# A graph kernel's edge loop: zero products at its start, attention columns and left-half turns inside it

## The reference

```
h = x @ W + b
adj[row, col] = 1; adj[col, row] = 1; adj += eye; adj /= max(row_sum, 1)
out = dw[0] * h; cur = h
for i in range(3):
    cur = adj @ cur
    out += dw[i + 1] * cur
x = layernorm(x + relu(out))
```

## Time and profile before

| | us |
|---|---|
| median of three runs | 394.62 |
| the profiled execution | 393.99 |
| its span, first to last instruction | 392.1 |
| PE busy | 366.8 (94%) |
| DVE busy | 281.6 (72%) |
| ACT busy | 239.0 (61%) |
| mean granted PE clock | 0.991 |

### The profile page before, as it was taken

One profiled execution on the slowest core, in us unless ns is written; L12 is line 12 of the kernel. 1 busy time (PEld: TensorE's weight loads), 2 busy tenths in 40 slices (PEclk: granted clock), 3 DMA queues, 4 the chain that ended last, 5 costly groups with the idle time before them and its releaser, 6 DMA issues.

```text
span 392.1 us, 7757 instructions
## 1 busy us (share of the span) xinstructions
PE 366.8 (94%) x2704; PEld 215.5 (55%) x2704; DVE 281.6 (72%) x595; ACT 239.0 (61%) x419; POOL 104.1 (27%) x97
## 2 busy tenths in 40 slices
PE   1799998999999999999999999999899999999990
PEld 0344456544444444444444444444358889999990
DVE  7999989729994775206755555564695978999984
ACT  9789998495722255202661011367866999999444
POOL 5611000059910167300792000277200000112110
PEclk9999999999999999999999999999999999999996
DMA  5960006006000000000243000034203111310005
GB/s 179 390 196 3 0 3 214 3 1 216 0 0 2 0 0 3 3 0 2 54 98 63 0 2 2 10 72 80 55 1 112 47 61 59 107 55 3 4 3 217
DMA packets 27446, 22.70 MB, mean 58 GB/s; under 512 B 19536, under 2 KB 19728, under 8 KB 27408
## 3 DMA queue, kind: packets, MB, share of 16 engines
q1 hardware_dynamic: 26544, 19.06, 16.2%
q10 hardware_dynamic: 864, 3.15, 2.4%
HBM read 15.87 MB, written 2.13 MB: 46 GB/s over the span
## 4 chain that ended last, share of the span: by engine, by line
PE 83%; ACT 6%; DVE 6%; issue 2%; DMA 1%; DVEq 0%; POOL 0%; ACTq 0%
PE ps L755 20%; PE ps L1114 14%; PE ps L1055 8%; PE ps L964 7%; PE ps L1005 7%; PE ps L927 7%; PE ps L918 7%; PE ps L788 4%; PE ps L908 4%; PE ps L897 3%; ACT cts L499 2%; PE ps L809 2%; ACT cts L507 1%; DVE adj L1357 1%; PE ps L824 1%
## 5 line engine op out<-in xcount | busy, mean ns | idle before, releaser
L755 PE MATMUL ps<-big,xTs 128*128 128x512 f16 x384 | 84.3, 379 | 0.3 <-DMA xTs<-big 0.3
L755 PEld LDWEIGHTS ps<-big,xTs 128*128 (+1 forms) x384 | 37.0, 98 | 43.9 <-issue 0.4
L664 ACT ACTIVATE big<-big,uvt 128x1024 bf16<-128x1024 f32 x55 | 58.7, 1143 | 0.0
L568 ACT ACTIVATE big<-xcur,nmr,rstd (+1 forms) x24 | 19.5, 813 | 34.0 <-DVE nmr L1383 34.0
L440 POOL TENSOR_TENSOR big<-xcur,big x16 | 18.5, 1156 | 61.3 <-ACT xcur L569 60.3
L788 PE MATMUL ps<-big,xTs 128*128 128x512 f32 x64 | 33.8, 628 | 0.0
L474 ACT ACTIVATE big<-ps 128x512 f16<-128x512 f32 (+2 forms) x17 | 9.7, 568 | 35.3 <-PE ps L755 30.9
L457 POOL TENSOR_TENSOR xcur<-xcur,c 128x512 f32<-128x512 f32 x6 | 7.1, 1183 | 89.4 <-DVE c L1586 89.4
L410 POOL TENSOR_TENSOR big<-xTs,big 128x2048 f16<-128x2048 f32 x4 | 16.2, 4084 | 52.8 <-ACT big L474 52.8
L1055 PE MATMUL ps<-big,cst 128*128 128x260 f16 x256 | 29.8, 275 | 0.0
L964 PE MATMUL ps<-cst,big 128*128 128x512 f16 x128 | 27.8, 379 | 0.1
(11 more groups left out here) (212 smaller groups left out, 689.0 us busy)
## 6 DMA issues: line engine op xcount, KB each, us to landing
big<-u_rows ACTq DMA_DIRECT2D x6, 512.0 KB, 3.7
xTs<-in_xT SPq DMA_DIRECT2D x2, 1024.0 KB, 9.3
xcur<-in_x SPq DMA_DIRECT2D x1, 2048.0 KB, 17.8
out<-xcur SPq DMA_DIRECT2D x8, 256.0 KB, 2.5
big<-in_W SPq DMA_DIRECT2D x1, 1024.0 KB, 6.0
cts<-in_W3T SPq DMA_DIRECT2D x1, 1024.0 KB, 13.3
xTs<-in_W1T SPq DMA_DIRECT2D x1, 1024.0 KB, 5.4
xTs<-in_wc SPq DMA_DIRECT2D x1, 1024.0 KB, 8.2
```

What stands on the lines that cost most here:

```text
L664: act.activation(above[:, a % AHEAD, :], uf[:, h % 2], ACT.Relu, scale=BIG, bias=vb[:, j, h:h + 1]).then_inc(S["above_in"], 1)
L755: return mm(bank, lhs(k)[a], rhs(k)[b], start=start and k == 0 and n == 0, stop=stop and k == KT - 1 and n == 2)
```

## The change

Seven things, in the order of the program:

1. `blank`, a zeroed piece of the W1 slot, feeds 19 matmuls of 128x512 on PE that nobody reads (`warm`): eight first, two and five around the key transposes, two behind each of quads 0 and 1.
2. The products are spread evenly over quads 2 to 26. xT comes in three transfers (the first 128 nodes apart), and the banks of the product tiles are a list.
3. Four column blocks of the attention columns stand behind the products of quads 14 to 17; ACT copies the result (`columns_in`) behind its relu of quad 19. w3t moves from cts to the wn slot.
4. Edge groups from 48 on have window bases of at least 512 (`low`, `first_i[:, 3]`), so columns below 512 are final when window 47 is added.
5. ACT casts the left half of c32 in four pieces behind its last relu, before the loop's end on DVE; PE turns blocks 0 to 3 from it behind quad 31. The right half is cast behind the last add: tiles 0 to 3 by DVE in two pieces, tiles 4 to 7 by ACT.
6. From quad 14 on, DVE makes the lo-hots of quads 16, 21, 26, 31 (before: 15, 21, 27).
7. ACT's squares of w3t come behind the last eviction.

```diff
-H_FROM = 4
-H_TO = 31
-H_LATE = 32
+H_FROM = 2
+H_TO = 27
 LO_TURN = 14
+WARM = (8, 2, 5, 2)
+COLUMNS_FROM = 14
+H_BANKS = (2, 3, 4, 5, 3, 4, 5, 3)
+XT_NODES = ((0, P), (P, HALF), (HALF, N))
...
-CAST_COLS = ((0, 256), (256, 512), (512, 1024))
-CT_BANKS = (0, 1, 5)
+LEFT_GROUP = 48
+CT_BANKS = (2, 5, 2, 5, 0, 1, 2, 5)
...
-            return q > 1 and (q % 2 == 0 if q < LO_TURN else q % 6 != 3)
+            return q > 1 and (q % 2 == 0 if q < LO_TURN else q % 5 != 1)
...
-                return NT * KT * (i - H_FROM) * (i + H_LATE) // ((H_TO - H_FROM) * (H_TO + H_LATE))
+                return NT * KT * (i - H_FROM) // (H_TO - H_FROM)
...
+                if mine[i - 1] < COLUMNS_FROM + KT + 1 <= q:
+                    act.wait_ge(S["wa_done"], 1)
+                    act.wait_ge(S["wba_in"], 1)
+                    copy(abT[:], ps[:, 2, 0:256].rearrange("p (k c) -> p k c", c=64)[:, :, 0:VCOL + H], WSCALE).then_inc(S["columns_in"], 1)
...
+            act.wait_ge(S["win_free"], LEFT_GROUP)
+            for j in range(0, NT, 2):
+                copy(cst[:, j:j + 2, 0:HALF], c32[:, j:j + 2, 0:HALF]).then_inc(S["cst_left"], 1)
...
+            evict_turned(0)
+            evict_turned(1)
+            act.wait_ge(S["win_free"], NG)
+            for j in (4, 6):
+                copy(cst[:, j:j + 2, HALF:N], c32[:, j:j + 2, HALF:N]).then_inc(S["cst_act"], 1)
+            for t in range(2, NT):
+                evict_turned(t)
...
+            def warm(n):
+
+                for _ in range(n):
+                    mm(ps[:, 4, :], blank[:, 0:P], blank, start=True, stop=True)
...
-                    pe.wait_ge(S["acc0"], t - 3)
-                    pe.wait_ge(S["h_lo"], t - 3)
+                    pe.wait_ge(S["acc0"], t - 2)
+                    pe.wait_ge(S["h_lo"], t - 2)
...
+                if q < H_FROM:
+                    warm(WARM[3])
...
-            pe.wait_ge(S["w_in5"], 16)
-            pe.wait_ge(S["small_in"], SMALL)
-            pe.wait_ge(S["h_lo"], 5)
-            pe.wait_ge(S["acc0"], 5)
-            attention_columns(range(KT)).then_inc(S["wa_done"], 1)
+                if q == COLUMNS_FROM:
+                    pe.wait_ge(S["w_in5"], 16)
+                    pe.wait_ge(S["small_in"], SMALL)
+                    pe.wait_ge(S["h_lo"], 1)
+                    pe.wait_ge(S["acc0"], 1)
+                if 0 <= q - COLUMNS_FROM < KT:
+                    attention_columns(q - COLUMNS_FROM)
...
+            pe.wait_ge(S["cst_left"], NT // 2)
+            pe.wait_ge(S["columns_in"], 1)
+            ct_block(0).then_inc(S["ct_done"], 1)
+            pe.wait_ge(S["acc0"], NT - 1)
+            pe.wait_ge(S["h_lo"], NT - 1)
+            ct_block(1).then_inc(S["ct_done"], 1)
+            for t in range(2, 4):
+                pe.wait_ge(S["cts_ready"], t - 1)
+                ct_block(t).then_inc(S["ct_done"], 1)
...
-                if 0 < j < NT - 3:
-                    ct_block(j + 3)
+                if j < 4:
+                    pe.wait_ge(S["cst_act"], 2)
+                    pe.wait_ge(S["cst_dve"], 2)
+                    if j >= 2:
+                        pe.wait_ge(S["cts_ready"], j + 1)
+                    ct_block(j + 4).then_inc(S["ct_done"], 1)
...
+            def cast_right(j):
+                dve.tensor_copy(cst[:, j:j + 2, HALF:N], c32[:, j:j + 2, HALF:N]).then_inc(S["cst_dve"], 1)
+
             dve.wait_ge(S["win_free"], NG)
-            for c0, c1 in CAST_COLS[0:2]:
-                dve.tensor_copy(cst[:, CA:NT, c0:c1], c32[:, CA:NT, c0:c1]).then_inc(S["cst_dve"], 1)
-            for t in range(tiles_low, NT):
-                h_lower(t)
+            cast_right(0)
...
-                if t == 1:
-                    dve.tensor_copy(cst[:, 2:5, c0:c1], c32[:, 2:5, c0:c1]).then_inc(S["cst_dve"], 1)
+                if t == 0:
+                    cast_right(2)
+                    for n in range(tiles_low, NT):
+                        h_lower(n)
```

More of the change, by code:

```diff
@@ L68 @@
 LN16 = 2.772588722239781
-CA = 3
 HT = NT // 2 - 1
@@ L183, in build @@
         base = sb("base", [NG, 1], F32)
-        first_i = sb("first_i", [1, 3, NG], I32)
+        low = sb("low", [NG, 1], F32)
+        first_i = sb("first_i", [1, 4, NG], I32)
         packed = sb("packed", [1, NG // 3 + 1], I32)
@@ L316, in _ @@
             sp.dma_start(w0raw, W0.rearrange("(k p) n -> p k n", p=P)).then_inc(S["w_in0"], 16)
-            for half in range(2):
-                nodes = slice(half * HALF, (half + 1) * HALF)
-                sp.dma_start(xT32[:, :, nodes], xT.rearrange("(k p) n -> p k n", p=P)[:, :, nodes]).then_inc(S[f"xT_in{half}"], 16)
+            for i, (n0, n1) in enumerate(XT_NODES):
+                sp.dma_start(xT32[:, :, n0:n1], xT.rearrange("(k p) n -> p k n", p=P)[:, :, n0:n1]).then_inc(S[f"xT_in{i}"], 16)
             sp.dma_start(w3t, W3T.rearrange("(k p) n -> p k n", p=P)).then_inc(S["w_in5"], 16)
@@ L776, in _ @@
             ins.then_inc(S["tr"], 1)
+            warm(WARM[2])
             def h_part(t, k):
+                if k == 0 and t == 1:
+                    pe.wait_ge(S["xT_in1"], 16)
                 if k == 0 and t == 2:
@@ L818, in far_columns, with attention_columns @@
                 pe.transpose(ps[0:1, 4, 0:NG], far_at[0:NG, 0:1], id32[0:NG, 0:NG]).then_inc(S["tr"], 1)
-            def attention_columns(ks):
-                for k in ks:
-                    for j in range(KT):
-                        ins = mm(ps[:, 2, k * 64:k * 64 + VCOL + H], w3t[:, j, k * P:(k + 1) * P], abT[:, j, :],
-                                 start=j == 0, stop=j == KT - 1)
-                return ins
+            def attention_columns(k):
+                for j in range(KT):
+                    ins = mm(ps[:, 2, k * 64:k * 64 + VCOL + H], w3t[:, j, k * P:(k + 1) * P], abT[:, j, :],
+                             start=j == 0, stop=j == KT - 1)
+                if k == KT - 1:
+                    ins.then_inc(S["wa_done"], 1)
             def attention_bias():
@@ L1204, in link @@
                 dve.wait_ge(S["link"], links[0])
+            dve.memset(blank, 0.0).then_inc(S["blank_in"], 1)
             dve.wait_ge(S["cols"], 2)
@@ L1343, in _ @@
                 dve.wait_ge(S["far_cast"], NT)
+                for t in range(4):
+                    dve.wait_ge(S["far_turn"], t + 1)
+                    dve.tensor_copy(cts[:, t, :], bank16(LEFT_AGAIN[t])).then_inc(S["far_turned"], 1)
+                dve.wait_ge(S["far_turned"], 4)
             dve.wait_ge(S["const_ready"], 12)
-            c0, c1 = CAST_COLS[2]
-            dve.tensor_copy(cst[:, 0:2, c0:c1], c32[:, 0:2, c0:c1]).then_inc(S["cst_dve"], 1)
             for t in range(NT):
```

97 lines of the change are left out of this document (45 added, 52 removed).

## The result

| | before | changed |
|---|---|---|
| median | 394.48 us (394.15 to 397.08, 4 runs) | 398.48 us (396.45, 396.58, 400.38, 400.38) |
| ratio of medians, interval | 1 | 1.0101 [1.0067, 1.0134] |
| profiled execution | 393.99, span 392.1 | 396.58, span 394.7 |
| mean granted clock of it | 0.991 | 0.985 |

The change costs about 1%. The forecast was 395.2 within 391.9 to 398.0; the median lies 0.5 outside. The times lie in steps of about 1.7 us (396.5, 398.3, 400.0 to 400.4); half of the experiments ask what those steps are.

What follows compares the result with a forecast made beforehand. PE was taken to bind the loop up to quad 18, then ACT's chain to step 1. Work removed behind the loop against a loop ending 2.8 later nets +0.6 on the median 394.62: 395.2, range 391.9 to 398.0.

Steps and rivals of the forecast that it cites:

- The sum up to quad 6: Edge loop's start on PE: five products, windows, far columns and one wait after quad 2; quad 6 starts at about 18.0.
- Quad 17's columns: Middle of the edge loop: PE's products, windows and four column blocks from quad 6 sum to 20.8, ending at 38.8.
- ACT's wait: Edge loop, behind quad 19's relu: ACT waits for the columns it copies, 34.85 to 38.85, 4.0 us.
- The last add: End of the edge loop on DVE: 23.6 us of work from 39.05, ending at 62.65.
- First product of step 1: Behind the loop: first product with the adjacency at 66.5, against 65.50 before, with ACT ending the chain.
- The net of +0.6: Up to step 1's second half: it starts at 82.15 instead of 81.51, and all behind shifts alike.
- comparison of tile 0: Behind the loop on DVE: starts at 64.95 after ACT's casts, turns and first eviction; 1.55 before the first product.
- Rival one: Middle of the loop: PE does not bind, ACT's wait vanishes, DVE decides, comparison 3.8 earlier: 391.4; chance 0.24.
- Rival three: Edge loop: DVE's busy time is partly waits, so the loop ends some 2 us before rival one's: 389.4; chance 0.05.
- a new gap behind 82: After step 1's second half starts: nothing new expected; a gap there would be wrong in kind. No size given.
- Rival 2b: Loop's thin end, from about 53.7: clock falls, step 1 starts at 1.2 GHz, 2.2 plus 0.3: 397.7; chance 0.23 with 2a.
- Rival 2a: Loop's start: zeros leave the clock low, five first products cost 0.85 more each, up to 4 us; chance 0.23 with 2b.

Runs made afterwards that it cites:

- e10: The changed kernel timed and traced once more, nothing altered: 400.0 us, ratio 1.0133.
- e6: e2 with H_TO = 29 instead of 27, spreading the 32 products over quads 2 to 28: 395.56 us, ratio 1.0008.
- e1: The kernel before with 51 transposes put into the far branch's body, which is never entered: 397.08 us, ratio 1.0057.
- e2: The changed kernel with 16 more matmuls in the far branch's body, never entered: 396.37 us, ratio 1.0026.
- e4: e2 with ACT's four left casts waiting for the last window instead of window 48: 401.17 us, ratio 1.0157.
- e7: The changed kernel without its 19 products of zeros, 35 unexecuted ones in the far branch keeping the later program's place as in e2: 398.16 us, ratio 1.0086.
- e13: The changed kernel with 5 further products meant for PE's wait near 280, which stood at 300 instead: 400.63 us, ratio 1.0149.
- e16: The changed kernel with the attention loop's first pass written out and 6 products in PE's wait of 1.6 us: 398.2 us, ratio 1.01.
- e14: The kernel before with 5 further products meant for PE's wait near 280, which stood at 300 instead: 395.67 us, ratio 1.0032.
- e17: The kernel before with the attention loop's first pass written out and 5 products in PE's wait of 1.23 us: 394.06 us, ratio 0.998.
- e3: The changed kernel with 16 more executed products of zeros, two behind each of quads 27 to 31 and six ahead of the first turn: 394.62 us, ratio 1.0001.

## Why the prediction was wrong, and where it was right

**Loop and opening: right.** First real product forecast at 11.65 with 0.90; it came at 11.77 with 1.10 (later ones 0.92). The sum up to quad 6 gives 17.75 where the text says about 18.0; it started at 18.14. Quad 17's columns end at 38.59 (38.8). ACT's wait, the row of waits from 8 to 70 us that answers to the earlier trace rows:

```profile
ACT abT L475 <- PE ps L843: 3.1, 1, 3.1
```

3.1 us against 4.0 forecast. The last add, with its row answering to the earlier trace rows:

```profile
62.00 0.50 DVE L1296 TENSOR_TENSOR c<-c,ps 128x328 f32 x1 [0.20 <-DVE c L1296]
```

ends at 62.50 (62.65). First product of step 1 at 66.18 (66.5), L941 at 81.94 (82.15). The net of +0.6 up to here was +0.43.

The order of limits was right, but the closeness at 66.2 is in part luck. ACT began its left casts at 57.63 where the sum had 59.2, and the comparison of tile 0, forecast at 64.95, came 1.2 us sooner:

```profile
63.77 1.23 DVE L1398 SCALAR_TENSOR_TENSOR adj<-cst,cts 128x1024 f16<-128x1024 f16 x1 [0.55 <-ACT cts L475]
```

From there to the first product it took 2.41 us where 1.55 was put (2.18 in e10), and the two misses nearly cancel. DVE had 0.55 us to spare ahead of this comparison, not over 1.

Rival one, PE not binding the middle, fell: PE was busy without a gap from 13.40 to 38.59. Rival three fell with it. The run nearest to it is e6, with ACT's wait down to 0.3: its step 1 started 0.92 earlier (65.26), so the 3.8 us put on this rival look too high.

**The gap: the step that failed.** The sum ended at L908 with +0.6 and took all behind it as a shift. The prediction's last line called a new gap behind 82 "wrong in kind", and this is what came: 2.02 us, shown by e1 and e2 to need only the 51 matmuls that the change adds to PE's program (19 zeros and 32 turns in the unentered body). The prediction priced the order of instructions, and put what their number does to the code behind at nothing. No rival had it. A smaller term was put at nothing as well: PE's wait near 280 is 0.36 longer, 1.58 or 1.59 for ACT in every trace of the changed kernel without a filler there, 1.23 in the kernel before; why is not known.

**The clock: priced, but rated too low and placed once.** Rival 2b said thin work at the loop's end lets the clock fall, 2.5 us, chance 0.23. The fall came in every trace of the changed kernel's loop without extra zeros (the changed kernel, e2, e4 to e7, e10, e13, e16). Where it reached the first products of step 1 (3.57 against 1.89 us, L941 at 83.52) its price was 1.6; in the profiled run it ended before them and the eight took 1.89. Its argument against, that the earlier trace rows keep 1.00 in 58.90 to 65.50, was from one execution: in the three other traces of that loop (e1, e14, e17) the clock falls at 62.4. Rival 2a did not come, since the zeros raised the clock in time; e7 shows two slow products and 1.6 us without them, where "up to 4" was put. The second fall at 282 is in no line of the prediction.

**The sum by what was measured.** 393.99 + 0.43 + 2.02 + 0.36 (PE's wait at 280) = 396.8, against 396.58 in the profiled run. At about 1.7 each, one costly fall gives 398.3 and two give 400.0, which are the steps seen. The first median, 398.48, is the middle between two runs at 396.5 and two at 400.38; the latter were not traced, and only their mean clocks, 0.977 and 0.978, speak for two falls. So of the 3.3 us between forecast and median 2.0 are the gap, and the rest is, as far as is known, the clock and the longer wait.

The Trainium skill ("TensorE: Matmul & The Clock Gate", section "What's actually happening") has the low level as the default that activity lifts. The runs agree for products of zeros: behind them the first real product took 1.10 us, without them 1.96 (e7), and e3's sixteen kept the clock at 1.00 from 62 to 64 where e2 had 0.64.

## What to carry to other kernels

A change that adds instructions to an engine's program, executed or not, moves everything behind them, and here that alone cost or gave back 2 us: compare the "issue" waits of untouched stretches before and after, and try a few dummy instructions in an unentered body before judging the change. When runs of one kernel lie in steps, compare their mean granted clocks, and try to fill PE's waits ahead of dense products (here 1.6 us); a single profiled execution may be one without the fall. Fillers belong in the pass of the loop that waits, which the timeline tells and the code's last call does not.

## What the runs showed of the hardware that was not expected

- A gap on PE, 1.7 to 2.6 us in six traces and at most 0.7 in fourteen, that instructions which are never executed bring (e1) and take away (e2). In five of the six the long piece comes four or five products behind a taken branch.
- The granted clock fell behind PE's wait near 280 (0.59 and 0.56 in e10's rows from 282 to 286) in four traces of the seventeen without the filler in that wait, and in none of the three with it. All four (e4, e7, e10, e13) are of the fourteen with the wait of 1.58 or 1.59 for ACT, none of the three with 1.23. Each such fall costs 1.69 us.
- It also fell while PE was busy without a gap. In e1, ahead of the fall and in it:

```profile
60.00:62.00 2.00, 2.00 (x20) 2.00 (x20) 2.00 (x4) 2.00 (x4) 0.00 (x0) 1.00 0.79 281
62.00:64.00 2.00, 2.00 (x19) 2.00 (x19) 1.70 (x3) 0.67 (x3) 0.00 (x0) 0.59 0.93 317
64.00:66.00 2.00, 2.00 (x23) 1.98 (x20) 1.07 (x1) 2.00 (x3) 0.00 (x0) 0.56 0.95 366
```

PE had the small products of 40 columns there, with a weight load each. The kernel before ran the same products in its profiled execution with the clock at 1.00, so a full busy share tells neither that the clock stays up nor that it falls.
